# Attention values of three of the four head-group pairs projected in quarters inside the turns instead of before them

## The reference

```
def proj(W):
    y = jnp.einsum('btc,dc->btd', x, W)
    return y.reshape(B, T, N_HEADS, HEAD_DIM).transpose(0, 2, 1, 3)
q, k, v = (proj(Wq), proj(Wk), proj(Wv))
att = jnp.einsum('bhqd,bhkd->bhqk', q, k) * scale
att = jnp.where(causal[None, None], att, -jnp.inf)
att = jax.nn.softmax(att, axis=-1)
out = jnp.einsum('bhqk,bhkd->bhqd', att, v)
return jnp.einsum('btc,dc->btd', out.transpose(0, 2, 1, 3).reshape(B, T, C), Wo)
```

## Time and profile before

| | us |
|---|---|
| median of 3 runs (lowest to highest) | 2296.11 (2289.29 to 2298.18) |
| the profiled execution's own time | 2295.74 |
| its span, first to last instruction | 2294.0 |
| first attention, prologue, then turns 0 to 7 | 46.8, then 284.5 |
| second attention, prologue, then turns 0 to 7 | 36.6, then 292.2 |
| mean granted TensorE clock | 0.894 of full |

### The profile page before, as it was taken

One profiled execution on the slowest core, in us unless ns is written; L12 is line 12 of the kernel. 1 busy time (PEld: TensorE's weight loads), 2 busy tenths in 40 slices (PEclk: granted clock), 3 DMA queues, 4 the chain that ended last, 5 costly groups with the idle time before them and its releaser, 6 DMA issues. The chain is left out here.

```text
span 2294.0 us, 28363 instructions
## 1 busy us (share of the span) xinstructions
PE 1928.2 (84%) x9864; PEld 1246.2 (54%) x9864; DVE 1597.7 (70%) x3418; ACT 882.4 (38%) x1657; POOL 474.3 (21%) x354
## 2 busy tenths in 40 slices
PE   7999997899999987956766377455889999999998
PEld 4644443688888855434433233232354444379997
DVE  4578982545444354789999999998367887266775
ACT  2267773222222223430121111101326766446775
POOL 1012211633131030001001101110011221114765
PEclk9689998899999999978887788777988997989999
DMA  5123431311010011100000000000032342137885
GB/s 171 22 50 66 87 63 52 110 56 55 18 54 1 0 56 34 58 0 10 10 1 9 19 0 10 9 0 0 24 56 50 66 86 44 34 113 230 233 236 121
DMA packets 60158, 132.73 MB, mean 58 GB/s; under 512 B 18952, under 2 KB 29960, under 8 KB 57216
## 3 DMA queue, kind: packets, MB, share of 16 engines
q1 hardware_dynamic: 50688, 118.17, 18.9%
q0 software_dynamic: 8832, 12.16, 3.2%
q10 hardware_dynamic: 512, 0.79, 0.2%
HBM read 91.27 MB, written 10.98 MB: 45 GB/s over the span
## 5 line engine op out<-in xcount | busy, mean ns | idle before, releaser
L805 DVE CUSTOM_DVE_ANT_0 pair<-pair,a_mask 128x512 f32<-128x512 f32 (+3 forms) x768 | 407.4, 587 | 117.5 <-PE pair L616 115.4
L771 ACT ACTIVATE a_prob<-pair 128x512 f32<-128x512 f32 (+3 forms) x768 | 330.5, 490 | 179.1 <-PE pair L643 176.9
L616 PE MATMUL pair<-a_kx,a_qx 48*128 48x512 f32 (+3 forms) x768 | 249.0, 416 | 15.2 <-DVE a_mx_raw L805 7.9
L643 PE MATMUL pair<-a_qx,a_kx 64*128 64x512 f32 (+3 forms) x768 | 249.3, 433 | 9.2 <-ACT a_prob L771 9.2
L643 PEld LDWEIGHTS pair<-a_qx,a_kx 64*128 64x128 f32 x768 | 119.5, 198 | 188.0 <-ACT a_prob L771 137.6
L1042 DVE TENSOR_TENSOR m_h<-pair,m_g 128x512 f32<-128x512 f32 x96 | 66.4, 691 | 211.0 <-PE pair L865 209.8
L1424 PE MATMUL pair<-h_stream,r_w_kz 128*128 128x512 f32 x192 | 104.1, 695 | 118.5 <-DVE r_region L1830 113.3
L863 PE MATMUL pair<-m_x_hi,m_w_lo 128*128 128x512 f32 x448 | 178.4, 398 | 26.6 <-POOL m_w_lo L927 24.5
L657 PE MATMUL pair<-a_prob,a_v 128*32 128x512 f32 (+3 forms) x1536 | 179.3, 541 | 6.9 <-ACT a_prob L771 4.0
L555 POOL TENSOR_SCALAR_AFFINE_SELECT a_prob<-a_prob 128x512 f32<-128x512 f32 x128 | 89.1, 696 | 433.2 <-ACT a_prob L771 433.2
L864 PE MATMUL pair<-m_x_hi,m_w_hi 128*128 128x512 f32 x448 | 177.2, 396 | 0.0
(11 more groups left out here) (316 smaller groups left out, 4118.7 us busy)
## 6 DMA issues: line engine op xcount, KB each, us to landing
mx_raw<-in_L_ffn_experts SPq DMA_DIRECT2D x69, 512.0 KB
m_raw<-in_L_cond_experts SPq DMA_DIRECT2D x18, 1024.0 KB, 5.0
a_qx<-a_comp SPq DMA_DIRECT2D x104, 96.0 KB, 2.8
a_kx<-a_comp SPq DMA_DIRECT2D x48, 192.0 KB, 4.4
a_factor<-a_inverses SPq DMA_DIRECT2D x56, 128.0 KB, 2.8
r_w_ring<-in_r_q_w SPq DMA_DIRECT2D x8, 512.0 KB, 4.0
m_raw<-in_L_cond_experts SPq DMA_DIRECT2D x6, 512.0 KB, 3.6
token_rows<-mx_h_rows SPq DMA_DIRECT2D x2, 1040.0 KB, 8.0
```

The lines of the kernel that those rows point to most:

```text
L616: nc.tensor.matmul(first_bank[t % FR][:, 0:c1 - c0], qx[r, m % 2, a // 2, i * P:(i + 1) * P], kx[r, m % 3, a // 2, c0:c1], start=True, sto ...
L643: nc.tensor.matmul(score_bank[t % SR][:, q0:TT], kx[r, n % 3, a // 2, j * P:(j + 1) * P], qx[r, n % 2, a // 2, h * TT + q0:(h + 1) * TT], ...
L771: nc.scalar.activation(prob[:, i % RING, a, q0:TT], score_bank[t % SR][:, q0:TT], ACT.Exp, scale=SCALE).then_inc(s["b_exp"], 1)
L805: nc.vector.tensor_tensor_reduce(out=first_bank[t % FR][:, 0:cols], in0=first_bank[t % FR][:, 0:cols], in1=mask[:, m0:m0 + cols], scale=1. ...
```

## The change

The values of pair 0 are projected as before in the prologue, but in four quarters (`v0`, 4 matmuls or 8 instructions each, in one bank each), all ahead of the first of the firsts. The values of pairs 1 to 3 leave the prologue: a quarter stands at the end of step 3 and of step 8 of the turns 0 to 5, takes the shared bank, and is copied by ACT after the first score of the next step. `values` of turns 2 to 7 waits for the fourth quarter of its pair. The values' tile holds four groups instead of eight, in 32 columns for each head with 15 columns of zeros where it had 17 with none; the matmul reads 32 columns either way. POOL writes those zeros at the start. `FIRST` is now ordered token block by token block with the head innermost (0, 1, 2, 3), and `FIRSTS_AFTER`, `VALUES_AFTER`, `SMALL` and `NORM` have new numbers.

```diff
-VW = HD + 1
+VW = SLOT
+QUARTERS = 4
...
-FIRST = [(a, i, c_) for part in (range(4), range(4, QT)) for a in range(GH) for i in part for c_ in range(i // 4 + 1)]
+FIRST = [(a, i, c_) for part in (range(4), range(4, QT)) for i in part for c_ in range(i // 4 + 1) for a in (0, 1, 2, 3)]
...
-FIRSTS_AFTER = ((0, 2, 0, 3), (1, 3, 0, 0), (1, 2, 0, 0), (0, 0, 3, 0),
+FIRSTS_AFTER = ((1, 2, 0, 0), (2, 2, 0, 2), (0, 1, 1, 1), (2, 0, 1, 1),
...
-VALUES_AFTER = (1, 3, 3, 3, 1, 0, 1, 2, 3, 3, 2, 3)
+VALUES_AFTER = (3, 3, 3, 1, 0, 1, 2, 1, 2, 3, 2, 1)
...
-SMALL = (("max", 0, 1), None, None, None, ("qk", 2, 0), ("qk", 2, 1), ("max", 1, 0), None, None, None, None, None)
+SMALL = (("max", 0, 1), None, None, ("v", 0, 0), ("qk", 2, 0), ("max", 1, 0), None, ("qk", 2, 1), ("v", 0, 1), None, None, None)
...
-SHARED = ("qk", "max", "sums", "spread", "out")
+SHARED = ("qk", "v", "max", "sums", "spread", "out")
...
-    values = [(pair, v) for pair in range(NG // 2) for v in range(2)]
+    for v in range(QUARTERS):
+        order += [("v0", v), ("v0_use", v)]
     for f in range(NF):
         order.append(("first", 0, f))
...
-        if f % 5 == 2 and values:
-            order += [("v", *values[0]), ("v_use", *values[0])]
-            values = values[1:]
...
+            elif what == "v":
+                entry = (what, n // 2 + 1, 2 * (n % 2) + y)
...
-        v_flat = c.sb(f"{tag}_v", [P, NG * QT * GH * VW + SLOT - VW], ctx=ctx)
-        v_sb = v_flat[:, 0:NG * QT * GH * VW].rearrange("p (n j c) -> p n j c", n=NG, j=QT)
+        v_sb = c.sb(f"{tag}_v", [P, 4, QT, GH * VW], ctx=ctx)
...
-                nc.gpsimd.memset(v_flat[:, NG * QT * GH * VW:], 0.0).then_inc(s["v_ones"], 1)
-                nc.gpsimd.memset(v_sb[:, :, :, :].rearrange("p x t (a s) -> p (x t a) s", s=VW)[:, :, HD:VW], 1.0)\
+                nc.gpsimd.memset(v_sb[:, :, :, :].rearrange("p x t (a s) -> p (x t a) s", s=VW)[:, :, HD:HD + 1], 1.0)\
+                    .then_inc(s["v_ones"], 1)
+                nc.gpsimd.memset(v_sb[:, :, :, :].rearrange("p x t (a s) -> p (x t a) s", s=VW)[:, :, HD + 1:VW], 0.0)\
                     .then_inc(s["v_ones"], 1)
...
+                def values_of(bank, pair, v):
+                    m = 2 * pair
+                    for t in range(QT // QUARTERS):
+                        for k in range(KD):
+                            last = nc.tensor.matmul(bank[:, t * P:(t + 1) * P], c.h[:, k, time(m, (QT // QUARTERS * v + t) * P, P)],
+                                                    w[:, m % GROUPS, 1, k, :], start=k == 0, stop=k == KD - 1)
+                    return last
+
+                def v_first(v):
+                    pe.wait_ge(s["used"], used("qk", 1, 1))
+                    values_of(v_banks[v], 0, v).then_inc(s["v0_mm"], 1)
+
                 def v_projection(pair, v):
...
+                    values_of(take("v", pair, v), pair, v).then_inc(s["vp"], 1)
...
                     pe.wait_ge(s["b_exp"], (n * NS + i + 1) * GH)
+                    if i == 0 and n > 1:
+                        pe.wait_ge(s["used"], used("v", n // 2, QUARTERS - 1))
...
+                def copy_quarter(bank, pair, v):
+                    n = QT // QUARTERS
                     for x in range(2):
                         last = nc.scalar.activation(
...
+                            v_sb[:, (2 * pair + x) % 4, n * v:n * v + n, :].rearrange("p t (a s) -> p t a s", s=VW)[:, :, :, 0:HD],
+                            bank[:, 0:n * P].rearrange("p (t x a s) -> p t x a s", t=n, x=2, s=HD)[:, :, x, :, :], ACT.Copy)
+                    return last
```

More of the change, by code:

```diff
@@ L244 @@
 PACKED = NG - 2
-NORM = {2: 0, 5: 1, 8: 2, 10: 3, 11: 4}
+NORM = {1: 0, 2: 1, 4: 2, 6: 3, 8: 4}
 NORM_LAST = {1: 0, 2: 1, 4: 2, 5: 3, 6: 4, 8: 5}
@@ L329, in turn @@
                 entry = (what, x, y)
+            elif what == "v":
+                entry = (what, n // 2 + 1, 2 * (n % 2) + y)
             else:
                 entry = (what, n + x, y)
-            if entry[1] < NG:
+            if entry[1] < (NG // 2 if what == "v" else NG):
                 order.append(entry)
@@ L386, in bank_of @@
         return score_bank[early[entry]] if entry in early else shared_bank[BANK_OF[entry] % SB]
-    def v_bank(pair, v):
-        return v_banks[(2 * pair + v) % len(v_banks)]
     def used(*entry):
@@ L518, in out_weights @@
                     sp.wait_ge(s["proj"], NG * HALF)
[L519 removed]
+                    sp.wait_ge(s["vp"], (NG // 2 - 1) * QUARTERS)
                     sp.dma_start(wo, A[w_out]).then_inc(s["ow"], 16)
@@ L585, in qk_projection @@
                     last.then_inc(s["proj"], 1)
-                def v_projection(pair, v):
-                    m = 2 * pair
-                    task = 2 * pair + v
-                    pe.wait_ge(s["used"], used("qk", 1, 1))
-                    if task >= len(v_banks):
-                        pe.wait_ge(s["v_used"], task - len(v_banks) + 1)
-                    bank = v_bank(pair, v)
-                    for t in range(4):
-                        for k in range(KD):
-                            last = nc.tensor.matmul(bank[:, t * P:(t + 1) * P], c.h[:, k, time(m, (4 * v + t) * P, P)],
-                                                    w[:, m % GROUPS, 1, k, :], start=k == 0, stop=k == KD - 1)
-                    last.then_inc(s["vp"], 1)
+                def values_of(bank, pair, v):
[8 more added lines that the diff above has]
+                    values_of(v_banks[v], 0, v).then_inc(s["v0_mm"], 1)
+                def v_projection(pair, v):
+                    values_of(take("v", pair, v), pair, v).then_inc(s["vp"], 1)
                 def first(m, t):
@@ L636, in scores @@
                         pe.wait_ge(s["v_ones"], 2)
-                        pe.wait_ge(s["v_used"], NG)
+                        pe.wait_ge(s["v0_used"], QUARTERS)
                     if j == 0 and a == 0:
@@ L655, in values @@
                     for a in range(GH):
-                        v0 = ((n * QT + j) * GH + a) * VW
-                        last = nc.tensor.matmul(value_bank[quadrant(a), q0:TT], v_flat[:, v0:v0 + SLOT], prob[:, i % RING, a, q0:TT],
+                        r = slice(a * SLOT, a * SLOT + VW)
+                        last = nc.tensor.matmul(value_bank[r, q0:TT], v_sb[:, n % 4, j, a * VW:(a + 1) * VW], prob[:, i % RING, a, q0:TT],
                                                 start=j == 0, stop=j == 4 * h + 3)
@@ L712, in out_projection @@
                     last.then_inc(s["om"], 1)
-                does = {"qk": qk_projection, "v": v_projection, "first": first, "max": maxima, "scores": scores,
+                does = {"qk": qk_projection, "v0": v_first, "v": v_projection, "first": first, "max": maxima, "scores": scores,
                         "values": values, "sums": sums, "spread": spread, "out": out_projection, "begin": begin_out}
```

19 lines of the change are left out of this document (10 added, 9 removed).

## The result

The changed kernel takes 2377.93 us (median of 4 runs, 2370.45 to 2389.72), the kernel before 2295.12 us on the same chip (4 runs). The ratio is 1.0412 with a 95% interval of 1.0366 to 1.0457: 4% slower, where 2286 us and a range of 2267 to 2306 were predicted. The profiled execution took 2371.57 us.

A forecast was written before the change was run, and what follows sets the result against it. Turns were taken as bound by a dense PE stream holding waits, over a DVE floor, prologues as a chain of PE bursts and DVE stretches. Prologues -23.0, quarters +12.0, half clock +1.0 gave -10.0: 2286 us, range 2267 to 2306.

The forecast's parts named there:

- Prologues: Both attentions' prologues: four quarters, then DVE working through its maxima without a break, turn 0 starting earlier; -23.0 us.
- The lower end of this term: Smallest prologue gain, all bursts at half clock and 2 us of bubbles for each prologue: about -17 us.
- The turn's price: Two quarters in each of turns 0 to 5: +1.0 us a turn, +12.0 for twelve, ends -12 and +43.
- 0.5 to 1.5 us: Range for the price of a turn outside which the forecast fails above all, since it counts twelve times.
- the first rival: Turns' steps 3 and 8: quarters paid in full, ACT runs dry; 3.6 us a turn, 2317 us; chance 0.15.
- the copies in the path: Part of that rival: ACT's copies of the quarters stand between exponentials; all four, 1.5 us a turn.
- The half absorption: In the turns, waits absorb about half of a full-array burst, so two quarters of 2.05 us cost 1.0.
- The bound of +3.6: Upper end for a turn: the whole burst, 2.05 us, and all four ACT copies in the scores' path, 1.5.
- forecast of -10: Whole kernel: -23.0 prologues, +12.0 quarters in turns, +1.0 half clock in turn 0, giving 2286 us.
- the same place of return: Turn 0: full clock returns some 21 us in, after the first query and key projection; half clock adds +1.0 us together.
- the clock takes it back: Rival: lighter prologue keeps half clock longer, 13.7 us more at half per attention, +10.8 us, 2297 us; chance 0.17.
- Edits at nothing: POOL's longer zero writing, the values' new wait, the shared bank and NORM: no cost, or 0.4 us for the bank.

The follow-up runs named there:

- the old tables: Changed kernel with the earlier kernel's FIRST, FIRSTS_AFTER, VALUES_AFTER, NORM and places of second projection and maxima, quarters kept at steps 3 and 8: 2290.89 us, ratio 1.0008.
- the tables alone: Kernel before, all values in the prologue, with the new FIRST, FIRSTS_AFTER, VALUES_AFTER, NORM and places of projections and maxima: 2376.44 us, ratio 1.0397.
- filling the boundary: Changed kernel plus useless 128 x 128 identity matmuls ahead of 8 firsts a turn in steps 11 and 0: 2360.41 us, ratio 1.0312.
- filling a dense place: Changed kernel plus the same useless identity matmuls ahead of firsts 20 to 27, in steps 5 and 6: 2513.39 us, ratio 1.094.
- the quarters in the prologue: Kernel before with its prologue values in 16 quarters of 8 instructions, one after every third first, instead of 8 bursts of 16: 2290.99 us, ratio 0.9981.

## Why the prediction was wrong, point by point

**Prologues: right.** Turn 0 starts at 79.4 (predicted 80.1), DVE fills 97% of the stretch (over 95% predicted), and the values' burst took 6.41 us for its 32 instructions (5.9 taken); in the second attention it took 5.46 (5.0 taken), and turn 0 starts 30.2 us behind the values' start (29 predicted):

```profile
48.23 6.41 PE L590 MATMUL pair<-w_qkv,h_stream 128*128 128x128 f32 x32 [4.01 <-DVE a_prob L804]
...
54.94 0.30 DVE L815 CUSTOM_DVE_ANT_0 pair<-pair,a_mask 128x128 f32<-128x128 f32 x1 [6.76 <-PE pair L616]
```

17.3 and 7.1 us, 24.4 together, were gained, and -23.0 was forecast. That PE ran at half among the firsts (0.55 and 0.61) cost next to nothing, as said: DVE was the bound. In the burst ahead of them it did cost: 6.41 us instead of the 4.1 of the full clock. The lower end of this term was added up wrongly: with 4 us of bubbles it is 24.3 - 4.3 - 4.0 = 16, not 17.

**The turn's price: mis-sized.** A turn at the full clock lasts 35.3 us, 2.2 more than before and not 1.0; twelve of them are +26 instead of +12. That is outside the 0.5 to 1.5 us on which the forecast was said to hang, and over the 35 us named as the sign of the first rival, bursts in full, whose other part, the copies in the path, did not show. The half absorption read from turns 5 and 6 did not hold for the quarters: 2.2 us is the whole of their PE time at the full clock, 2.05. The bound of +3.6 held it. With the old tables, where the quarters are nearly all that is new in a turn, it is 2.3. In the changed kernel part of it can be the tables, as said at the tables alone. The Trainium skill, "TensorEngine Tiling (Array Packing)", section "Key Properties", has changes of the tiling mode drain TensorE. 2.2 against 2.05 leaves 0.15 us for four changes if the bursts are paid in full; if part of each burst fell into waits, that part could be the price of the changes, and no run here tells the two apart. With prologues at -24.4 and turns at +26.4 the change comes to +2, and the old tables measured 1.0008: 2 us. So with the clock as before the forecast of -10 would have been 12 us off, though inside its range.

**The clock: the step that failed.** The sentence was "I expect the same place of return, some 21 us into the turn, and no other change". The place of return in turn 0 held (22.1 us into it); "no other change" did not. The rival "the clock takes it back" (chance 0.17) named the clock, but laid it to the thinner prologue, with one more stretch of 13.7 us in each attention and 10.8 us in all; the runs showed half clock in ten of the twelve turns 0 to 5, where the kernel before had it in four, and brought by the tables. The granted clocks of the turns, by the rows above, give 2 x (0.19 x 327.1 + 0.26 x 350.7) = 307 us at half instead of 2 x (0.07 x 284.5 + 0.11 x 292.2) = 104, so 203 more. (The stretches themselves, added up over the turns, give 310 and 104.) A turn of 44.5 us with 23.9 at half is 9.2 longer than one of 35.3, so 1 us at half costs 0.385; 203 x 0.385 = 78. With 12 x 2.2 = 26 for the quarters that is 104, and the turns grew by 101.1. Over the whole span, 218 us more at half, nearly all of them in the turns.

Why it was missed: I costed the change of order by the pairs that could ride together and by waits, as if it could only move work within a turn. But the earlier trace rows had the clock fall at 141.60, amid a turn, with PE busy for all of the 13.70 us behind it, and turn 5 of the second attention had 0.82. That said that the order stood near an edge, and it should have become a rival with a fall in every turn: 12 x 5.4 = 65 us, from the 38.50 against 33.10 of the earlier trace rows. The Trainium skill, "TensorE: Matmul & The Clock Gate", section "What's actually happening", says that activity releases the throttle and puts the ramp at under 1% of a typical span. The first agrees with the return behind a dense projection. The second is about the ramp and no measure for this kernel: here the falls come in the middle of work, with PE busy for 2.79 of 3.40 us, and 30% of the span (707 of 2370 us) is at half.

**Shown:** the loss is in the tables and not in the quarters; in the changed kernel it appears as half clock in the turns, in some of its variants also as a longer turn at the full clock; filling the boundary gives part of it back, filling a dense place makes it worse. **Only argued:** that the five wide maxima of step 11 are what thins PE there, and that this thin place is what brings the falls. **Open:** which property of the stream holds the clock. Putting single tables in or back gave no one table; the same thin boundary was followed by a fall in most turns and by none ahead of turn 3; and the busy share alone doesn't tell: the last 3.4 us ahead of before's fall at 1885.8 had PE at 3.30 us, with 25 matmuls:

```profile
1882.40:1885.80 3.40, 3.30 (x25) 1.71 (x24) 2.85 (x15) 3.24 (x7) 0.61 (x1) 1.00 0.71 118
```

**Edits at nothing: right.** POOL's longer constant took 1.76 us from 38.99 on, and the values' burst, which began at 48.23, covered what it delayed; a quarter's copy took 274 ns on ACT. The waits of ACT for scores in a turn rose from 9.4 us (old tables) to 17.4 (turn 5 of the changed kernel), and DVE's for firsts from 5.8 to 14.2: both turns have the same instructions but for their order, so most of this is PE at half. The rows of waits, who waited for whom, total us, times, longest, of the changed kernel's turn 5 and of the old tables' turn at full clock:

```profile
ACT a_prob L781 <- PE pair L643: 17.4, 16, 2.5
DVE pair L815 <- PE pair L616: 14.2, 13, 2.9
```

```profile
ACT a_prob L781 <- PE pair L643: 9.4, 12, 1.9
DVE pair L815 <- PE pair L616: 5.8, 8, 1.5
```

## What to carry to other kernels

Where PE is the bound and its granted clock sits between its levels, a new order of instructions is also a change of clock: list the falls and rises of the clock before, price one fall in a turn, and give a rival in which every turn has one. Change work and order in separate steps: here the gain of 24 us in the prologue was real and the quarters' price in the turns took it up, and the loss came from tables that had no need to change with them. When the same order is tried in several variants, read a turn at the full clock and the us at half apart, since two kernels of the same time can differ in both. A stretch in which another engine paces PE costs nothing at its own place, and may, as argued here, be paid in the 20 us behind it.

## What the runs showed of the hardware

- Extra PE work can lower the granted clock: 56 matmuls an attention in a dense place took the mean from 0.851 to between 0.816 and 0.836 in its four executions, and turns from 44 to 51 us and more; at the turn's boundary they raised it to 0.885.
- The clock can stay at half under full load: the second prologue with short bursts (8 instructions every third first) stayed there for all of its 52.1 us with PE busy for 51.33, while before's with 16-instruction bursts had 0.93. The grain of the bursts doesn't decide it: in the first prologue the short ones had 0.78 and the long ones 0.65.
- A fall needs no long idle stretch of PE, and the same instructions need not bring one: the boundary ahead of turn 4 (2.79 of 3.40 us busy) was followed by 23.9 us at half, the one ahead of turn 3 (2.86 of 3.40) by none.
- Turn and clock can keep step: turns 1 to 5 of the changed kernel's second attention had 44.3 to 44.5 us, with 23.9 at half in each. The same instructions in attention one gave two such turns, two with no half clock and one with 13.7 us.
- One kernel's executions differ with it: the 10 runs of the quarters in the prologue lie between 2263 and 2305 us; the two fastest had a mean clock of 0.905, the slowest 0.883. That is 2 x 0.022 x 2283 = 100 us at half for 42 us, 0.42 for each, near the 0.385 read from the turns.
